# A fused two-layer transformer step: the roll layer in seven groups of four images and two of two, with spectra multiplied by three real products

## The chip, the cores and the metric

The kernel runs on one core of one Trainium2 chip. The metric is the device time of one execution in microseconds (us): 1072.96 is the median of 3 runs (1072.81 to 1073.27).

## What is computed

32 images give 36 patch tokens each, to which 32 text tokens are appended: S = 68 tokens per image, 2176 rows of 256 numbers, held as 17 tiles of 128 rows. Two layers follow, each an attention and a mixture of experts. The change is in the attention of the second layer, the "roll layer":

```
z    = softmax over s of (x @ W_A.T) / 4           # 16 heads, one weight per token
roll = zp[:, :, (i - j) % S] * tril                # a causal convolution over the 68 tokens
out  = einsum('bhij,bjhd->bihd', roll, x @ W_V.T)
h    = h + out @ W_O.T + b_O
```

## The kernel before

All stages are written out by hand for the five engines: PE (matmul), ACT and DVE (elementwise), POOL (gathers) and SP (DMA issue), tied by semaphores. `roll_layer` (line 1471) also finishes the mixture before it: POOL gathers the 8 expert rows of each token (136 indirect DMAs, line 1606), and DVE adds them into `h` (`combine`, line 1919).

The convolution is done in the frequency domain. `forward` (line 1646) multiplies the values of two images (a pair, 512 columns) by a cosine and a sine matrix (68x68), `forward_mix` (line 1658) does so for the softmax weights, `multiply` (line 1965) forms on DVE the four real products of the two complex spectra, and `invert` (line 1672) sums the four, each by its inverse matrix, in `po`.

The 32 images go in NG = 8 groups of GI = 4 images (two pairs each), one group a step, in a pipeline of three stages: in step `i` group `g1 = i-1` is normalised, turned (`turn("in")`), and its logits and values are computed; group `g2 = i-2` goes through `forward`, `multiply`, `invert` and `project`; group `g3 = i-3` is added to `h`, normalised again, turned (`turn("out")`), given its expert logits (`choose`) and written to DRAM by SP (lines 1554 and 1555). There are NG + 3 = 11 steps, 0 to 10; steps 9 and 10 have no `g1`. Step `i` also combines the gathered rows of the tiles of group `i`.

Each engine takes its instructions in the order written in its own loop over the steps (PE from line 1742, ACT from 1870, DVE from 1987). On PE there stand `fill`, `fill_values` and `fill_mid` (lines 1688 to 1705) between the stages: bf16 matmuls of 512 columns whose result nothing reads, 17 of them in a full step. POOL's gathers are paced by waits on PE's progress (`first_half`, `second_half`). An fp32 matmul shows as two records in the trace.

Of the kernel before, what the change touches and what calls it, by code (L numbers as in the profile page):

```python
# [71 lines left out]
def constants():  # L72
# [28 lines left out]
        "inv_re": (np.cos(turn).T * weight),  # L101
# [1369 lines left out]
def roll_layer(nc, a, k, r, wt, y_rows, shared_up, shared_down):  # L1471
# [8 lines left out]
    CP = 2 * S  # L1480
    YR = 4

    def tiles_in(g):
        if not 0 <= g < NG:
            return []
        return list(range(0 if g == 0 else 2 * g + 1, 2 * g + 3))

    def tiles_out(g):
        if not 0 <= g < NG:
            return []  # L1490
        return list(range(2 * g, NT if g == NG - 1 else 2 * g + 2))

    def pairs_out(g):
        ts = tiles_out(g)
        return [(ts[n] // 2, ts[n:n + 2]) for n in range(0, len(ts), 2)]
# [11 lines left out]
    with ExitStack() as st:  # L1507
# [9 lines left out]
        zf = sb("zf", [NF, 2, 2, GI, H])  # L1517
        v = sb("v", [S, 2, GI, D])
        term = sb("term", [NF, 2, 4, 2 * D])
# [23 lines left out]
        with nc.Block() as block:  # L1543
# [16 lines left out]
            def _(pool):  # L1560
# [4 lines left out]
                def first_half(g, kk):  # L1565
                    if kk == 1 and g >= 2:
                        pool.wait_ge(projected, pairs_out(g - 2)[-1][0] + 1)
# [43 lines left out]
            def _(pe):  # L1611
# [9 lines left out]
                def mix_logits(g):  # L1621
                    pe.wait_ge(turn_moved, turn_at["in", tiles_in(g)[-1]] + 1)
                    if g:
                        pe.wait_ge(zf_moved, g)
                    for c in range(DC):
                        mm = nc.tensor.matmul(pz[0:H, 0:GC], late["w_a"][:, c, :], xT[:, c, g * GC:(g + 1) * GC],
                                              start=(c == 0), stop=(c == DC - 1))
                    mm.then_inc(z_done, 1)

                def values(g, p):  # L1630
                    j = g * 2 + p
# [9 lines left out]
                def forward(g, p, part):  # L1641
                    n = (g * 2 + p) * 2 + part
                    pe.wait_ge(v_moved, g * 2 + p + 1)
                    if n >= 3:
                        pe.wait_ge(terms, 2 * (n - 2))
                    nc.tensor.matmul(pf[0:NF, n % 3, :], fwd[part], v[:, g % 2, 2 * p:2 * p + 2, :].rearrange("s b n -> s (b n)"),
                                     start=True, stop=True).then_inc(forwarded, 1)

                def turn_mix(g):
                    pe.wait_ge(z_normed, g + 1)  # L1650
                    for b in range(GI):
# [3 lines left out]
                def forward_mix(g):  # L1655
                    pe.wait_ge(zt_moved, g + 1)
                    for part in range(2):
                        mm = nc.tensor.matmul(pz[0:NF, (1 + part) * GI * H:(2 + part) * GI * H], fwd[part],
                                              zt[:, :, :].rearrange("s b m -> s (b m)"), start=True, stop=True)
                    mm.then_inc(zf_done, 1)  # L1660

                def invert(g, p):
                    j = g * 2 + p
                    pe.wait_ge(terms, (j + 1) * 4)
                    if j:
                        pe.wait_ge(out_moved, j)
                    for c in range(DC):
                        for b in range(2):
                            for i in range(4):
                                for half in range(2):  # L1670
# [3 lines left out]
                                        term[:, j % 2, i, lo:lo + P // 2], inv[i], start=(i == 0), stop=(i == 3))  # L1674
                    mm.then_inc(inverted, 1)

                def project(g, m, ts):
                    pe.wait_ge(out_moved, 2 * (g + 1))
                    if m:
                        pe.wait_ge(proj_added, m)  # L1680
                    for s, t in enumerate(ts):
# [12 lines left out]
                def fill_values(g, n):  # L1694
                    pe.wait_ge(v_moved, g * 2 + 2)
# [4 lines left out]
                def fill_mid(g, n):  # L1700
                    if not 0 <= g < NG:
# [40 lines left out]
                for i in range(STEPS):  # L1742
# [34 lines left out]
                    if has1:  # L1777
                        values(g1, 1)
# [8 lines left out]
                    if has2:  # L1787
                        invert(g2, 1)
                        fill_values(g1, 2)
                    if has1:  # L1790
                        turn_mix(g1)
                    for m, ts in pairs_out(g2):
                        project(g2, m, ts)
# [6 lines left out]
            def _(act):  # L1800
                def move_out(g, p):
                    j = g * 2 + p
# [4 lines left out]
                def move_mix(g):  # L1807
# [3 lines left out]
                    nc.scalar.activation(z[:, :, :].rearrange("m b s -> m (b s)"), pz[0:H, 0:GC], ACT.Copy,  # L1811
                                         scale=float(HD) ** -0.5).then_inc(z_moved, 1)

                def move_values(g, p):
                    if g >= 2:
                        act.wait_ge(forwarded, (g - 1) * 4)
                    act.wait_ge(v_done, g * 2 + p + 1)
# [27 lines left out]
                def exp(g):  # L1845
                    act.wait_ge(z_shifted, g + 1)
                    nc.scalar.activation(z[:, :, :], z[:, :, :], ACT.Exp).then_inc(exped, 1)

                def move_mix_turned(g):
                    act.wait_ge(z_turned, g + 1)  # L1850
                    nc.scalar.activation(zt[:, :, :].rearrange("s b m -> s (b m)"), pz[0:S, 0:GI * H], ACT.Copy)\
                        .then_inc(zt_moved, 1)

                def move_mix_forwarded(g):
                    act.wait_ge(zf_done, g + 1)
                    if g >= 2:
                        act.wait_ge(terms, (g - 1) * 8)
                    nc.scalar.activation(zf[:, g % 2, :, :, :].rearrange("f r b m -> f (r b m)"), pz[0:NF, GI * H:3 * GI * H],
# [11 lines left out]
                for i in range(STEPS):  # L1870
# [3 lines left out]
                    if has2 and not has1:  # L1874
                        move_out(g2, 0)
                        move_out(g2, 1)
# [18 lines left out]
                    if has1:  # L1895
                        move_values(g1, 1)
                        exp(g1)
                    if has2:
                        move_out(g2, 0)
                        move_out(g2, 1)  # L1900
# [5 lines left out]
            def _(dve):  # L1906
# [29 lines left out]
                def mix_shift(g):  # L1936
                    dve.wait_ge(z_moved, g + 1)
                    link(nc.vector.tensor_reduce(zpeak[:, :], z[:, :, :], AX.X, ALU.max))
                    nc.vector.tensor_tensor(z[:, :, :], z[:, :, :], zpeak[:, :].unsqueeze(2).broadcast_to([H, GI, S]),
                                            ALU.subtract).then_inc(z_shifted, 1)  # L1940

                def mix_norm(g):
                    dve.wait_ge(exped, g + 1)
                    link(nc.vector.tensor_reduce(zsum[:, :], z[:, :, :], AX.X, ALU.add))
                    link(nc.vector.reciprocal(zsum[:, :], zsum[:, :]))
                    nc.vector.tensor_tensor(z[:, :, :], z[:, :, :], zsum[:, :].unsqueeze(2).broadcast_to([H, GI, S]),
                                            ALU.mult).then_inc(z_normed, 1)

                def add_projected(m, ts):
                    dve.wait_ge(projected, m + 1)  # L1950
# [4 lines left out]
                def multiply(g, p):  # L1955
                    j = g * 2 + p
# [4 lines left out]
                    for i, part, zpart in ((0, 0, 0), (2, 0, 1), (1, 1, 1), (3, 1, 0)):  # L1961
                        n = j * 2 + part
                        dve.wait_ge(forwarded, n + 1)
                        weights = zf[:, g % 2, zpart, 2 * p:2 * p + 2, :].rearrange("f b m -> f (b m)")
                        mm = nc.vector.tensor_tensor(term[:, s, i, :].rearrange("f (m n) -> f m n", n=HD),
                                                     pf[0:NF, n % 3, :].rearrange("f (m n) -> f m n", n=HD),
# [21 lines left out]
                for i in range(STEPS):  # L1988
# [5 lines left out]
                    for m, ts in pairs_out(g3):  # L1994
                        add_projected(m, ts)
                    if has2 and not has1:
                        multiply(g2, 0)
                        multiply(g2, 1)
                        for t in outs:
                            dve.wait_ge(proj_added, t // 2 + 1)  # L2000
                            measure("out", t)
                        scale("out", outs)
                        continue
# [425 lines left out]
```

## Time and profile before

| | us |
|---|---|
| median of 3 runs | 1072.96 |
| the profiled execution, its own time | 1074.8 |
| its span, first to last instruction | 1073.0 |
| roll layer, from its first gather to its last DVE instruction | 634.5 to 875.1 |
| of it step 3 to the end | 718 to 875 |
| PE busy over the span | 939.0 (88%) |
| DVE busy | 582.3 (54%) |
| ACT busy | 412.1 (38%) |
| POOL busy | 519.4 (48%) |

Times in the rows are us from the start of the span. In a timeline row the first number is the start, the second the length until the last of its records ends; matmuls overlap, so the cost of a group is read from its start to the next group's start. The bracket gives the idle time before it on that engine and who ended it. PEclk is the granted TensorE clock: 1.00 is 2.4 GHz, 0.50 is 1.2 GHz.

### The profile page before, as it was taken

How to read it: one execution, taken by the hardware profiler on the slowest of the kernel's cores; microseconds unless marked ns; L12 is line 12 of the kernel's file. 1: busy time of each engine (PE TensorE's matmuls, PEld its weight loads, DVE VectorE, ACT ScalarE, POOL GpSimd, SP SyncE). 2: the span in 40 equal slices, each digit the busy share in tenths (PEclk: the TensorE clock that was granted, in tenths of full speed). 3: DMA queues.
4: the chain of work that ended last, by engine and by line, in shares of the span. 5: the costliest groups of instructions: out<-in, count | busy, mean ns of one | idle time of the engine just before them, and what ended most of it. 6: DMA issues, size and time to landing. Idle time of an engine off the chain costs nothing. (4 is left out here: it accounts for less than half of the span.)

```text
span 1073.0 us, 29482 instructions
## 1 busy us (share of the span) xinstructions
PE 939.0 (88%) x10318; PEld 741.5 (69%) x10318; DVE 582.3 (54%) x1439; ACT 412.1 (38%) x1094; POOL 519.4 (48%) x714
## 2 busy tenths in 40 slices
PE   8699999978824999999999986599999954999996
PEld 6457777767722888888888875255665634888895
DVE  1768888855995677533333325678877432111111
ACT  2357667743334343443434311233333222333331
POOL 0045565620603777777677617777772002343332
PEclk9879999979967999999999989789999976999998
DMA  7010000002003988887888723335463047466750
GB/s 253 2 44 2 0 0 0 1 2 84 1 0 109 307 267 271 279 243 214 254 261 253 231 80 103 103 104 140 122 214 125 21 153 261 138 224 236 282 154 25
DMA packets 79820, 149.28 MB, mean 139 GB/s; under 512 B 18892, under 2 KB 53327, under 8 KB 75760
## 3 DMA queue, kind: packets, MB, share of 16 engines
q1 hardware_dynamic: 34768, 77.15, 21.4%
q0 software_dynamic: 17712, 47.88, 15.7%
q10 hardware_dynamic: 27248, 23.09, 6.4%
q8 instruction: 50, 0.82, 0.3%
q14 instruction: 42, 0.34, 0.1%
HBM read 200.22 MB, written 31.73 MB: 216 GB/s over the span
## 5 line engine op out<-in xcount | busy, mean ns | idle before, releaser
L1311 POOL DMA_INDIRECT x_x<-m_x_rows,x_idx x170 | 165.8, 975 | 75.2 <-issue 35.9
L1337 PE MATMUL x_pup<-x_xt,x_w 128*128 128x128 f32 (+1 forms) x2176 | 184.7, 251 | 0.0
L1337 PEld LDWEIGHTS x_pup<-x_xt,x_w 128*128 128x128 f32 (+1 forms) x2176 | 168.7, 166 | 6.0 <-issue 5.9
L1606 POOL DMA_INDIRECT rl_y<-m_y_rows,rl_idx x136 | 132.8, 976 | 46.3 <-issue 36.9
L1407 DVE TENSOR_TENSOR x_hid<-x_gate,x_pup 128x128 f32<-128x128 f32 x170 | 48.9, 288 | 148.3 <-ACT x_gate L1379 144.3
L1351 PE MATMUL x_pdown<-x_w,x_hid 128*128 128x256 f32 (+1 forms) x408 | 104.2, 389 | 0.3 <-DVE x_y L1414 0.3
L1375 ACT ACTIVATE x_xt<-x_pturn 128x256 f32<-128x256 f32 x170 | 65.3, 384 | 88.9 <-PE x_pturn L1322 86.0
L434 POOL TENSOR_TENSOR wa_probs<-wa_probs,wa_peak 68x544 f32<-68x544 f32 x64 | 69.9, 1092 | 58.7 <-DVE wa_peak L576 58.7
L2365 DVE TENSOR_TENSOR x_y<-x_pdown,x_b 128x256 f32<-128x256 f32 x21 | 8.9, 425 | 151.3 <-PE x_pdown L2321 151.3
L2351 ACT ACTIVATE x_hid<-x_pup,x_b 128x128 f32<-128x128 f32 (+1 forms) x200 | 52.9, 356 | 93.3 <-PE x_pup L2304 93.1
L1379 ACT ACTIVATE x_gate<-x_pup 128x128 f32<-128x128 f32 x170 | 47.2, 278 | 93.5 <-PE x_pup L1337 92.8
L1322 PE MATMUL x_pturn<-cst,x_x 128*128 128x128 f32 x340 | 68.3, 283 | 9.2 <-DMA x_x<-m_x_rows,x_idx 9.2
L1919 DVE SCALAR_TENSOR_TENSOR h<-rl_y,m_wt,h 128x256 f32<-128x256 f32 x136 | 66.1, 486 | 16.8 <-DMA rl_y<-m_y_rows,rl_idx 12.6
L1414 DVE COPY x_y<-x_pdown 128x256 f32<-128x256 f32 x170 | 71.3, 420 | 2.0 <-PE x_pdown L1351 0.5
L1322 PEld LDWEIGHTS x_pturn<-cst,x_x 128*128 128x128 f32 x340 | 45.4, 143 | 36.8 <-issue 13.1
L2260 POOL DMA_INDIRECT out_h<-x_y,m_ids_out x21 | 21.2, 1008 | 91.4 <-DVE x_y L2368 85.7
L620 ACT ACTIVATE wa_probs<-wa_probs 68x544 f32<-68x544 f32 x64 | 42.1, 658 | 46.4 <-POOL wa_probs L434 46.3
L1296 POOL COPY x_idx<-m_ids 128x1 uint32 (+1 forms) x170 | 37.0, 218 | 42.0 <-POOLq L904 40.9
L572 DVE TENSOR_TENSOR wa_probs<-wa_scores,cst 68x544 f32<-68x544 f32 x64 | 46.0, 719 | 10.0 <-PE wa_scores L530 7.6
L2304 PE MATMUL x_pup<-x_xt,late_w 128*128 128x128 f32 x384 | 48.0, 286 | 3.2 <-ACT x_xt L2341 1.9
L2304 PEld LDWEIGHTS x_pup<-x_xt,late_w 128*128 128x128 f32 x384 | 46.9, 201 | 5.6 <-issue 3.7
L1351 PEld LDWEIGHTS x_pdown<-x_w,x_hid 128*128 128x128 f32 (+1 forms) x408 | 48.1, 173 | 3.9 <-DVE x_hid L1407 0.6
(329 smaller groups left out, 1886.8 us busy)
## 6 DMA issues: line engine op xcount, KB each, us to landing
x_w<-in_experts SPq DMA_DIRECT2D x204, 384.0 KB
late_w<-in_w SPq DMA_DIRECT2D x28, 1024.0 KB, 14.5
m_y_rows<-x_y ACTq DMA_DIRECT2D x170, 128.0 KB
xT<-in_w SPq DMA_DIRECT2D x12, 1024.0 KB, 6.2
xn<-in_w SPq DMA_DIRECT2D x10, 1024.0 KB, 10.7
h<-in_w SPq DMA_DIRECT2D x10, 1024.0 KB, 14.7
m_x_rows<-xn SPq DMA_DIRECT2D x34, 128.0 KB, 1.9
x_x<-m_x_rows,x_idx POOLq DMA_INDIRECT x170, 3.1
```

The source lines that it names most:

```text
L434: nc.gpsimd.tensor_tensor(probs[:, slot4, :, :], probs[:, slot4, :, :], peak[:, slot2, :].unsqueeze(2).broadcast_to([S, HC, S]), ALU.subtr ...
L1311: nc.gpsimd.indirect_dma_start(x[:, s, :], None, x_rows, bass.IndirectOffsetOnAxis(ap=idx[:, s:s + 1], axis=0))\
L1322: mm = nc.tensor.transpose(pturn[:, bank, c * P:(c + 1) * P], x[:, s, c * P:(c + 1) * P], ident)
L1337: mm = nc.tensor.matmul(pup[rows:rows + wide, bank, m * P + side * wide:m * P + (side + 1) * wide], w[:, lane, first:first + wide], xt[:, ...
L1351: mm = nc.tensor.matmul(pdown[rows, s % 2, 0:D], hid[:, s, rows], w[:, lane, UP:W], start=True, stop=True)
L1375: nc.scalar.activation(xt[:, s, :], pturn[:, bank, 0:D], ACT.Copy).then_inc(turn_moved, 1)
L1407: nc.vector.tensor_tensor(hid[:, s, :], gate[:, s, :], pup[:, bank, P:2 * P], ALU.mult)\
L1414: nc.vector.tensor_copy(y[:, s, :], pdown[:, s % 2, 0:D]).then_inc(down_moved, 1)
L1606: nc.gpsimd.indirect_dma_start(y[:, t % YR, kk, :], None, y_rows, bass.IndirectOffsetOnAxis(ap=idx[:, n:n + 1], axis=0))\
L1919: nc.vector.scalar_tensor_tensor(h[:, t, :], y[:, t % YR, kk, :], wt[:, t, kk:kk + 1], h[:, t, :], ALU.mult, ALU.add).then_inc(added, 1)
L2304: mm = nc.tensor.matmul(pup[rows:rows + wide, s, half, to:to + wide], w1[l][:, c, first:first + wide], xt[:, s, at:at + wide], start=(c == ...
L2351: ins = nc.scalar.activation(hid[:, s, f, side * wide:(side + 1) * wide], pup[:, s, f // HB, at:at + wide], ACT.Gelu, bias=b1[:, l, f:f + 1])
```

## The change

The groups are now `SIZES = [4]*7 + [2]*2`: nine groups, twelve steps, the last two groups of one pair each. The tiles of a group follow from the running sum of images. Each spectrum product is formed from three real products in place of four: `forward` makes three parts (sum, cosine, sine) of each pair, `forward_mix` three, `multiply` three, and `invert` sums three. Each part has its own bank of `pf`. `project` takes one wait and one increment per group. The fills return at once for the two groups of two. The weights of the next stage (`NG - 4` in SP's loop) are issued behind group 4's rows in place of group 3's. The table of constants holds two 68x68 matrices more.

```
@@ constants
-        "inv_re": (np.cos(turn).T * weight),
+        "fwd_sum": np.cos(turn) - np.sin(turn),
+        "fwd_diff": -np.sin(turn) - np.cos(turn),
+        "inv_sum": (np.cos(turn).T - np.sin(turn).T) * weight,
@@ roll_layer
-    fwd = [k["const"]("fwd_re"), k["const"]("fwd_im")]
-    inv = [k["const"]("inv_re"), k["const"]("inv_neg"), k["const"]("inv_im"), k["const"]("inv_im")]
-    GI = 4
-    NG = B // GI
+    fwd = [k["const"](n) for n in ("fwd_sum", "fwd_re", "fwd_im")]
+    fwd_mix = [k["const"](n) for n in ("fwd_re", "fwd_diff", "fwd_sum")]
+    inv = [k["const"](n) for n in ("inv_sum", "inv_im", "inv_neg")]
+    PARTS = len(inv)
+    GI, PAIR = 4, 2
+    SIZES = [4] * 7 + [2] * 2
...
                 def forward(g, p, part):
-                    n = (g * 2 + p) * 2 + part
-                    pe.wait_ge(v_moved, g * 2 + p + 1)
-                    if n >= 3:
-                        pe.wait_ge(terms, 2 * (n - 2))
-                    nc.tensor.matmul(pf[0:NF, n % 3, :], fwd[part], ...
+                    n = pair_of(g, p) * PARTS + part
+                    pe.wait_ge(v_moved, pair_of(g, p) + 1)
+                    if n >= PARTS:
+                        pe.wait_ge(terms, n - PARTS + 1)
+                    nc.tensor.matmul(pf[0:NF, part, :], fwd[part], ...
...
-                            for i in range(4):
+                            for i in range(PARTS):
...
                 def fill(g, n):
+                    if NG - 2 <= g < NG:
+                        return
...
                 def fill_values(g, n):
-                    pe.wait_ge(v_moved, g * 2 + 2)
+                    if NG - 2 <= g < NG:
+                        return
+                    pe.wait_ge(v_moved, pairs_through(g))
...
                 def fill_mid(g, n):
-                    if not 0 <= g < NG:
+                    if not 0 <= g < NG - 2:
                         return fill(g, n)
@@ PE, the loop over the steps
                     if has2:
-                        forward(g2, 0, 0)
-                        forward(g2, 0, 1)
-                        forward(g2, 1, 0)
+                        for part in range(PARTS):
+                            forward(g2, 0, part)
...
                     if has2:
-                        forward(g2, 1, 1)
+                        for p in halves(g2)[1:]:
+                            for part in range(PARTS):
+                                forward(g2, p, part)
                     if has2 and not has1:
                         fill(g2 + 1, 8)
-                        invert(g2, 0)
-                        fill(g2 + 1, 4)
-                        invert(g2, 1)
-                        fill(g2 + 1, 2)
-                        for m, ts in pairs_out(g2):
-                            project(g2, m, ts)
+                        for p in halves(g2):
+                            invert(g2, p)
+                            fill(g2 + 1, 3)
+                        project(g2)
@@ DVE, multiply
-                    for i, part, zpart in ((0, 0, 0), (2, 0, 1), (1, 1, 1), (3, 1, 0)):
-                        n = j * 2 + part
-                        dve.wait_ge(forwarded, n + 1)
+                    for part in range(PARTS):
+                        dve.wait_ge(forwarded, j * PARTS + part + 1)
```

The order of PE in the middle of a full step, before (`rl_pz` from L1626 are the logits, `rl_pv` the values, `rl_pf` the forward products, `rl_pt` the turns, `rl_po` from L1672 the inverse; bf16 512-column rows are fills):

```order
L1626 MATMUL rl_pz<-xT,late_w_a 16x272 x2
L1637 MATMUL rl_pv<-late_w_v,xT 68x256 x4
L1646 MATMUL rl_pf<-rl_v,cst 68x512
L1618 MATMUL rl_pt<-cst,xn 128x128 x2
L1705 MATMUL rl_pz<-m_chosen_b,m_before_b 128x512
L1618 MATMUL rl_pt<-cst,xn 128x128 x2
L1705 MATMUL rl_pz<-m_chosen_b,m_before_b 128x512
L1637 MATMUL rl_pv<-late_w_v,xT 68x256 x4
L1712 MATMUL rl_po<-late_wr,rl_x 128x8 x4
L1705 MATMUL rl_pz<-m_chosen_b,m_before_b 128x512 x2
L1672 MATMUL rl_po<-cst,rl_term 64x68 x32
```

And now (the lines of the file have moved by 17 to 22):

```order
L1643 MATMUL rl_pz<-xT,late_w_a 16x272 x2
L1654 MATMUL rl_pv<-late_w_v,xT 68x256 x4
L1663 MATMUL rl_pf<-rl_v,cst 68x512 x3
L1635 MATMUL rl_pt<-cst,xn 128x128 x2
L1727 MATMUL rl_pz<-m_chosen_b,m_before_b 128x512
L1635 MATMUL rl_pt<-cst,xn 128x128 x2
L1727 MATMUL rl_pz<-m_chosen_b,m_before_b 128x512
L1654 MATMUL rl_pv<-late_w_v,xT 68x256 x4
L1734 MATMUL rl_po<-late_wr,rl_x 128x8 x4
L1727 MATMUL rl_pz<-m_chosen_b,m_before_b 128x512 x2
L1690 MATMUL rl_po<-cst,rl_term 64x68 x24
```

The one forward product in the middle of the step has become three, with the three at the step's start left as they were in number, and each of the two inverses of a step has 24 matmuls in place of 32. The fills stand where they stood.

The first step with a group of two as `g1` (step 8, `g2` still a group of four), on PE now:

```order
L1635 MATMUL rl_pt<-cst,xn 128x128 x2
L1643 MATMUL rl_pz<-xT,late_w_a 16x136 x2
L1654 MATMUL rl_pv<-late_w_v,xT 68x256 x4
L1663 MATMUL rl_pf<-rl_v,cst 68x512 x3
L1635 MATMUL rl_pt<-cst,xn 128x128 x4
L1734 MATMUL rl_po<-late_wr,rl_x 128x8 x4
L1690 MATMUL rl_po<-cst,rl_term 64x68 x48
L1669 MATMUL rl_pz<-cst,rl_z 68x16 x2
L1700 MATMUL rl_pr<-late_b_o,cst 128x256
L1702 MATMUL rl_pr<-late_w_o,xT 128x256 x2
```

Before, step 8 read as a full step does, with its 17 fills. Now the fills are gone, one tile is turned in, one pair of values is computed, and the two inverses follow each other directly.

## Rows read from the trace of the kernel before

**Rows 1.** Timeline of PE in one step: start us, us, instruction, [idle before <-releaser].
```profile
742.39 0.38 PE L1618 MATMUL rl_pt<-cst,xn 128*128 128x128 f32 x2
...
743.34 0.41 PE L1618 MATMUL rl_pt<-cst,xn 128*128 128x128 f32 x2 [0.35 <-ACT xT L1838]
...
744.23 1.09 PE L1626 MATMUL rl_pz<-xT,late_w_a 128*16 128x272 f32 x4
...
747.03 1.02 PE L1646 MATMUL rl_pf<-rl_v,cst 68*68 68x512 f32 x2
...
752.36 2.13 PE L1672 MATMUL rl_po<-cst,rl_term 68*64 68x68 f32 x64
...
754.41 0.61 PE L1705 MATMUL rl_pz<-m_chosen_b,m_before_b 128*128 128x512 bf16 x2
...
761.33 0.41 PE L1658 MATMUL rl_pz<-rl_zt,cst 68*68 68x64 f32 x4
...
761.58 0.60 PE L1697 MATMUL rl_pv<-m_chosen_b,m_before_b 128*128 128x512 bf16 x2
```

**Rows 2.** Timeline of DVE and ACT, the start of the next step.
```profile
762.50 0.16 DVE L1933 SCALAR_TENSOR_TENSOR rl_shift<-rl_mv,rl_rstd 128x2 f32<-128x2 f32 x1 [4.04 <-ACT rl_rstd L1826]
...
762.70 1.09 ACT L1832 ACTIVATE xn<-h,rl_shift,rl_rstd 128x256 f32<-128x256 f32 x2 [0.23 <-DVE rl_shift L1933]
...
764.40 2.48 DVE L1965 TENSOR_TENSOR rl_term<-rl_pf,rl_zf 68x512 f32<-68x512 f32 x4
```

**Rows 3.** Timeline of POOL, its last gather.
```profile
811.93 1.20 POOL L1606 DMA_INDIRECT rl_y<-m_y_rows,rl_idx  x1 [0.30 <-issue]
```

**Rows 4.** Busy time by engine over one step: length, PE, PEld, DVE, ACT, POOL, PEclk, DMA.
```profile
762.00:784.00 22.00, 21.26 (x210) 13.35 (x209) 17.29 (x40) 7.37 (x21) 16.82 (x18) 1.00 0.48 127
```

**Rows 5.** Timeline of PE from the last full step to the end of the layer.
```profile
828.59 2.74 PE L1646 MATMUL rl_pf<-rl_v,cst 68*68 68x512 f32 x6
...
846.98 0.70 PE L1682 MATMUL rl_pr<-late_b_o,cst 128*128 128x256 f32 x2
...
849.67 0.59 PE L1697 MATMUL rl_pv<-m_chosen_b,m_before_b 128*128 128x512 bf16 x2
...
850.78 3.63 PE L1646 MATMUL rl_pf<-rl_v,cst 68*68 68x512 f32 x8
...
854.25 1.89 PE L1692 MATMUL rl_pz<-m_chosen_b,m_before_b 128*128 128x512 bf16 x8
...
865.44 0.67 PE L1682 MATMUL rl_pr<-late_b_o,cst 128*128 128x256 f32 x2 [0.87 <-DVE h L1952]
...
866.81 0.38 PE L1618 MATMUL rl_pt<-cst,xn 128*128 128x128 f32 x2
```

**Rows 6.** Timeline of the SyncE queue: first weight load and last row write of the layer.
```profile
791.71 0.49 SPq L1550 DMA_DIRECT2D late_w<-in_w  x1
...
872.79 0.45 SPq L1555 DMA_DIRECT2D m_h_rows<-h  x1
```

**Rows 7.** Waits of the SyncE queue from 850 us on: total us, times, longest us.
```profile
SPq L1543 <- DMA m_h_rows<-h: 3.3, 1, 3.3
```

**Rows 8.** The page, section 6 (DMA issues): count, KB each, us to landing.
```profile
late_w<-in_w SPq DMA_DIRECT2D x28, 1024.0 KB, 14.5
```

**Rows 9.** Timeline of PE, beside two falls of its clock.
```profile
697.73 0.69 PE L1618 MATMUL rl_pt<-cst,xn 128*128 128x128 f32 x2 [3.66 <-ACT xn L1832]
...
704.81 1.02 PE L1646 MATMUL rl_pf<-rl_v,cst 68*68 68x512 f32 x2
...
873.27 1.51 PE L1712 MATMUL rl_po<-late_wr,rl_x 128*128 128x8 f32 x12
```

**Rows 10.** Busy time by engine, as rows 4, for stretches beside both falls.
```profile
697.00:700.00 3.00, 2.13 (x7) 1.00 (x7) 2.44 (x5) 1.79 (x4) 2.23 (x3) 0.50 0.38 115
...
874.00:874.50 0.50, 0.50 (x7) 0.50 (x7) 0.00 (x0) 0.00 (x0) 0.00 (x0) 0.93 0.31 105
874.50:875.00 0.50, 0.50 (x3) 0.24 (x3) 0.18 (x1) 0.00 (x0) 0.00 (x0) 0.50 0.00 0
```

More of the change, by code:

```diff
@@ L1474, in roll_layer @@
     ident = k["const"]("ident")
-    fwd = [k["const"]("fwd_re"), k["const"]("fwd_im")]
-    inv = [k["const"]("inv_re"), k["const"]("inv_neg"), k["const"]("inv_im"), k["const"]("inv_im")]
-    GI = 4
-    NG = B // GI
+    fwd = [k["const"](n) for n in ("fwd_sum", "fwd_re", "fwd_im")]
[4 more added lines that the diff above has]
+    SIZES = [4] * 7 + [2] * 2
+    assert sum(SIZES) == B
+    NG = len(SIZES)
+    FROM = [sum(SIZES[:g]) for g in range(NG + 1)]
     GC = GI * S
-    CP = 2 * S
+    CP = PAIR * S
     YR = 4
@@ L1485, in tiles_in @@
             return []
-        return list(range(0 if g == 0 else 2 * g + 1, 2 * g + 3))
+        return list(range(-(-FROM[g] * S // P), -(-FROM[g + 1] * S // P)))
     def tiles_out(g):
@@ L1490, in tiles_out, with halves, pair_of, pairs_through @@
             return []
[L1491 to L1495, printed above, removed]
+        return list(range(FROM[g] * S // P, FROM[g + 1] * S // P))
+    def halves(g):
+        return range(SIZES[g] // PAIR)
+    def pair_of(g, p):
+        return FROM[g] // PAIR + p
+    def pairs_through(g):
+        return FROM[g + 1] // PAIR
+    def cols_of(g):
+        return slice(FROM[g] * S, FROM[g + 1] * S)
+    assert all(len(tiles_out(g)) <= 2 for g in range(NG))
     STEPS = NG + 3
@@ L1650, in turn_mix @@
                     pe.wait_ge(z_normed, g + 1)
[L1651 removed]
+                    for b in range(SIZES[g]):
                         mm = nc.tensor.transpose(pz[0:S, b * H:(b + 1) * H], z[:, b, :], ident[0:H, 0:H])
@@ L1673, in invert, with project @@
                                         po[half * (P // 2):(half + 1) * (P // 2), (c * 2 + b) * S:(c * 2 + b + 1) * S],
-                                        term[:, j % 2, i, lo:lo + P // 2], inv[i], start=(i == 0), stop=(i == 3))
+                                        term[:, j % 2, i, lo:lo + P // 2], inv[i], start=(i == 0), stop=(i == PARTS - 1))
                     mm.then_inc(inverted, 1)
[L1677 to L1681, printed above, removed]
+                def project(g):
+                    pe.wait_ge(out_moved, pairs_through(g))
+                    if g:
+                        pe.wait_ge(proj_added, g)
+                    for s, t in enumerate(tiles_out(g)):
                         nc.tensor.matmul(pr[:, s, :], ident, late["b_o"][:, :], start=True, stop=False)
@@ L1777, in _ @@
                     if has1:
-                        values(g1, 1)
+                        for p in halves(g1)[1:]:
+                            values(g1, p)
                     for t in outs:
@@ L1787, in _ @@
                     if has2:
-                        invert(g2, 1)
-                        fill_values(g1, 2)
+                        for p in halves(g2)[1:]:
+                            invert(g2, p)
+                            fill_values(g1, 2)
                     if has1:
                         turn_mix(g1)
-                    for m, ts in pairs_out(g2):
-                        project(g2, m, ts)
+                    if has2:
+                        project(g2)
                     if has1:
@@ L1874, in _ @@
                     if has2 and not has1:
-                        move_out(g2, 0)
-                        move_out(g2, 1)
+                        for p in halves(g2):
+                            move_out(g2, p)
                         root("out", outs)
@@ L1895, in _ @@
                     if has1:
-                        move_values(g1, 1)
+                        for p in halves(g1)[1:]:
+                            move_values(g1, p)
                         exp(g1)
                     if has2:
-                        move_out(g2, 0)
-                        move_out(g2, 1)
+                        for p in halves(g2):
+                            move_out(g2, p)
                     if has1:
@@ L1993, in _ @@
                         scale("in", tiles_in(g1))
-                    for m, ts in pairs_out(g3):
-                        add_projected(m, ts)
+                    if outs:
+                        add_projected(g3)
                     if has2 and not has1:
-                        multiply(g2, 0)
-                        multiply(g2, 1)
+                        for p in halves(g2):
+                            multiply(g2, p)
+                        dve.wait_ge(proj_added, g3 + 1)
                         for t in outs:
-                            dve.wait_ge(proj_added, t // 2 + 1)
                             measure("out", t)
@@ L2019, in _ @@
                     if has2:
-                        multiply(g2, 1)
+                        for p in halves(g2)[1:]:
+                            multiply(g2, p)
                     if has1:
```

72 lines of the change are left out of this document (41 added, 31 removed).

## The prediction, made before the changed kernel had run

> **What bounds the kernel now.** The chain of waits that ended last lies in the expert stage behind the roll layer, so it says nothing of the change. I read the timeline of each engine inside the layer instead, then the busy time by engine of one step, then the clock.
>
> A full step takes 850.78 - 828.59 = 22.19 us from one step's first `forward` to the next one's [rows 5]. In a step PE is busy 21.26 of 22.00 us [rows 4]. It waits for 0.35 us behind the first turn in, until ACT has moved the tile [rows 1], and as long behind the first turn out; there is no other gap. DVE is busy 17.29 of the 22.00 us [rows 4] and stands still for 4.04 us until ACT gives it `rstd` [rows 2]; ACT stands behind PE's `forward_mix`, which ends PE's step. POOL's last gather is issued at 811.93 [rows 3], 0.30 us behind the one before it, and 63 us before the layer ends. So **PE's own list, fills included, sets the length of a step**: what is added to it is paid in full, what is taken from DVE is not seen.
>
> **The steps with a group of four: dearer.** Prices are from starts. Four `forward` products are 8 records and take 854.25 - 850.78 = 3.47 us [rows 5], 0.434 a record. An inverse is 64 records and takes 754.41 - 752.36 = 2.05 us [rows 1], 0.032 a record. `forward_mix` is 4 records in 761.58 - 761.33 = 0.25 us [rows 1], 0.06 a record.
> - `forward`: two pairs by one product more, 4 records, +1.73 us.
> - `invert`: twice 16 records fewer, -1.03 us.
> - `forward_mix`: one product more, 2 records, +0.12 us.
>
> Together +0.82 us a step. Steps 2 to 7 pay it (groups 0 to 5 in `forward`): **+4.9 us**. Step 2 pays too, though it begins late behind a gather: once PE starts its turns at 697.73 [rows 9] it runs on to the step's end.
>
> DVE saves one of four products a pair, 2.48 / 4 = 0.62 us [rows 2]. That goes into its wait of 4.04 us and is worth nothing. Moved or longer at no cost: the weights for the next stage are now issued a group later (before: from 791.71 [rows 6]), landing in 14.5 us [rows 8] where some 40 us are left; without that cover the layer's end would wait for the rest. ACT's copy of the mixed spectra grows by half; it runs under fills. The larger table of constants lands in the first stage, before its first reader.
>
> **The short end.** From step 8 on groups are short and have no fills, so PE's list no longer covers the round through ACT. Where one PE instruction needs what ACT must move from the one before, the pair costs 743.34 - 742.39 = 0.95 us in place of the 0.22 of a turn [rows 1]: 0.73 of waiting a round. I add work and rounds.
>
> Step 8 (before: 22.19). PE's work: six records of `forward` twice 2.60, turn in 0.22, logits half of 1.02 (744.23 to the values) is 0.51, values 747.03 - 744.23 - 1.02 = 1.78 [rows 1], two turns out 0.44, two `choose` 0.9 (of 1.51 for three [rows 9], two thirds and a little off for the overlap), two inverses of 48 records 3.08, `project` 849.67 - 846.98 = 2.69 [rows 5], the turns of the weights and `forward_mix` 0.43: 15.25. Rounds: turn in, turns out, between the inverses 0.73 each, the second `choose` 0.33, the move before `project` 0.6: 3.1. Together 18.35.
>
> Step 9 (before: 866.81 - 850.78 = 16.03 [rows 5], with two inverses, two `project`s and 14 fills). Now `g1` is the last group of two and `g2` has one pair: work 2.60 + 0.22 + 0.51 + 1.78 + 0.44 + 0.9 + 1.54 + 1.35 (`project` of one tile) + 0.37 = 9.7. Rounds: 0.73, then the turns out, which are late: ACT must normalise two tiles (1.09 [rows 2]) and move logits and values first, behind a DVE `scale` that stands behind `multiply`. I take 1.4 there, between 0.73 and 2.1. With 0.33 and 0.65: 3.1. Together 12.8.
>
> Step 10 and 11: `forward` 2.60, eight fills, the inverse, three fills, `project` of two tiles: 2.60 + 1.83 + 1.54 + 0.7 + 2.69 = 9.35. Then the last batch: the sum into `h`, measuring, `rstd`, normalising, row writes. Before, that ran from 866.81 to the end of the last issue at 872.79 + 0.45 = 873.24: 6.43 us with three tiles [rows 5, 6]. With two tiles it is one normalisation (0.55), one measuring (0.6) and two issues less, less what overlaps, and the sum of two tiles is now in it: 5.3.
>
> Sum of the end: 18.35 + 12.8 + 9.35 + 5.3 = 45.8; before 873.24 - 828.59 = 44.65 [rows 5, 6]. **+1.1 us**: the fills that go are eaten by the waits that come and by one step more. SP waits 3.3 us for that last write [rows 7], and the layer ends with it, so it stands for the end.
>
> **The clock.** PE runs at 1.00 through all full steps [rows 4]. After 3.66 us without work PE restarted at 0.50, the 1.2 GHz level, between 697 and 700 [rows 9, 10]. From there to the `forward` at 704.81 it took 7.08 us; the same stretch at full clock takes 747.03 - 742.39 = 4.64 [rows 1, 9]. So one fall costs 2.4 us of dense work. But a fall needs no long pause: at 874.5 the clock went to 0.50 with PE busy all the half microsecond before, on the twelve small `choose` records behind turns with gaps of 0.4 us [rows 9, 10]. In step 9 turns out, `choose` and a gap of 1.4 us stand together with no fill between them, the same mix. The trace of before has no such stretch inside the layer, so I bound it: 0 if the clock holds, 2.4 for a fall in dense work, 4.8 for one in step 8 as well. I take one fall, in step 9, nearest to the row at 874. A quarter of step 9 is waiting (3.1 of 12.8), which a slow clock doesn't lengthen: **+1.8 us**.
>
> The Trainium skill has two sections on this in "TensorE: Matmul & The Clock Gate". "HAM oscillation — how this bites in real kernels" ties the fall to long waits for data between groups of matmuls; by that alone a gap of 1.4 us would leave the clock up and the sum at 1079.0. "A second HAM failure mode: psum-queue depth-cycling" says that frequent short idles between groups also make the clock swing; by that the sum is the one I forecast. The fall at 874 agrees with the second.
>
> **The sum.** +4.9 +1.1 +1.8 = +7.8 us in the profiled span (1073.0; that execution took 1074.8 in all, 1.8 above the span). The parts outside the layer don't change, so the median of the runs moves as much: 1072.96 + 7.8 = **1080.8**.
>
> **Rivals.**
> - *The clock holds* (first section of the page; for it: the longest gap I add is under half of 3.66 us; against: 874). +6.0: 1079.0.
> - *It falls in step 8 too*, around the turns out and `choose`. Against: the inverses behind them are dense. +9.6: 1082.6.
> - *The short steps run without waits.* For: DVE has spare time, and PE may find each move already done. Then 6.2 us of rounds go: 4.9 + 1.1 - 6.2 = -0.2, 1072.8, no change. Against: the turn needs ACT's copy, and one copy is 0.73 away in every step of the trace.
> - *The other side: DVE, not PE, paces the steps.* Then three products in place of four take 0.62 us from each of the 14 pairs of the first seven groups, -8.7, and the extra `forward`s lie beside them: with the end +1.1, 1065.4. It decides where DVE's wait for `rstd` is nothing. Against: that wait is 4.04 us, and PE's whole idle is 0.7 a step.
>
> Over 0.2% (2.1 us, about what a measurement of this kernel can tell from no change) is faster below 1070.8 and slower above 1075.1.
>
> **How the numbers follow.** One fall of the clock 0.42, none 0.32, two 0.12, no waits 0.09, DVE 0.05. The first three are slower: 0.86, of which I take 0.01 off because all three could be 4 us too dear. Faster 0.07: the DVE case and a little of the one without waits. Same 0.08. The first three hold more than 8 in 10, from 1079.0 to 1082.6; the unknown rounds (some 3 us below, if half of them are covered) and the bounds of the clock stretch this to 1076.0 to 1084.0.
>
> **What the profile after would show.** Full steps of 23.0 us from `forward` to `forward`, PE without gaps but the two of 0.35, six records where two stood in the middle of the step and 48 in an inverse of some 1.54 us; DVE's wait for `rstd` grown from 4.04 to some 6 us. From step 8 on, steps of about 18, 13 and 9 us, PE with gaps of 0.6 to 1.5 us, and a stretch at 0.50 behind the turns out of step 9. I am wrong on the steps if they stay at 22.2 or shrink; on the end if from the `forward` of step 8 to the last row write there are not 45 to 49 us; on the clock if it stays at 1.00 up to the last `choose`.

## Result: slower by 1.35%, and the clock falls twice

| | before | after |
|---|---|---|
| median of 3 runs, us | 1072.96 (1072.81 to 1073.27) | 1089.43 (1082.34 to 1090.88) |
| ratio, 95% interval | | 1.0135 [1.0106, 1.0163] |
| span of the profiled execution, us | 1073.0 | 1087.6 |
| first `forward` of the layer, us | 691.34 | 690.21 |
| first `forward` of step 8, us | 828.59 | 832.78 |
| end of the last row write's issue, us | 873.24 | 887.27 |

The forecast was 1080.8 with a range of 1076.0 to 1084.0. The sign is right; the time is 5.4 us above the range. Ratios leave out two executions of the later runs that were far slower than the rest, of 4652.83 and 1163.24 us. The page of the changed kernel, sections 1 and 2 (busy tenths and granted clock in 40 slices):

```profile
PE 950.8 (87%) x10098; PEld 745.1 (69%) x10098; DVE 575.1 (53%) x1430; ACT 413.2 (38%) x1102; POOL 518.0 (48%) x714
PE   8699999978734999999999983899999965999996
PEclk9889999969967999999999997899999776999998
```

PE has 220 records fewer than before and is busy 11.8 us longer. Records differ in price, so that proves nothing yet, but the row of the clock shows where to look: in it the 32nd digit (843 to 870 us) is 7; before, the 32nd (832 to 858 us) was 9.

Timeline of PE in the changed kernel, one full step (compare [rows 1]):

```profile
740.32 2.74 PE L1663 MATMUL rl_pf<-rl_v,cst 68*68 68x512 f32 x6
...
743.85 0.41 PE L1635 MATMUL rl_pt<-cst,xn 128*128 128x128 f32 x2 [0.35 <-ACT xT L1862]
...
747.53 2.74 PE L1663 MATMUL rl_pf<-rl_v,cst 68*68 68x512 f32 x6
750.11 0.38 PE L1635 MATMUL rl_pt<-cst,xn 128*128 128x128 f32 x2
...
754.58 1.67 PE L1690 MATMUL rl_po<-cst,rl_term 68*64 68x68 f32 x48
756.17 0.61 PE L1727 MATMUL rl_pz<-m_chosen_b,m_before_b 128*128 128x512 bf16 x2
...
762.63 0.53 PE L1676 MATMUL rl_pz<-rl_zt,cst 68*68 68x64 f32 x6
763.00 0.60 PE L1719 MATMUL rl_pv<-m_chosen_b,m_before_b 128*128 128x512 bf16 x2
763.43 1.02 PE L1663 MATMUL rl_pf<-rl_v,cst 68*68 68x512 f32 x2
```

The step takes 763.43 - 740.32 = 23.11 us, 0.92 more than before's 22.19 [rows 5]; the only waits are still the two of 0.35 behind a first turn. The forecast had 23.0. Then the short end, where the forecast failed. Timeline of PE from step 8 to the end of step 10, and the last row write of SP:

```profile
832.78 2.74 PE L1663 MATMUL rl_pf<-rl_v,cst 68*68 68x512 f32 x6
...
842.09 0.41 PE L1635 MATMUL rl_pt<-cst,xn 128*128 128x128 f32 x2 [0.57 <-ACT rl_x L1867]
842.33 1.25 PE L1734 MATMUL rl_po<-late_wr,rl_x 128*128 128x8 f32 x8
843.51 1.66 PE L1690 MATMUL rl_po<-cst,rl_term 68*64 68x68 f32 x48
845.76 2.91 PE L1690 MATMUL rl_po<-cst,rl_term 68*64 68x68 f32 x48 [0.59 <-ACT xT L1827]
...
853.93 2.77 PE L1663 MATMUL rl_pf<-rl_v,cst 68*68 68x512 f32 x6
...
861.01 0.41 PE L1635 MATMUL rl_pt<-cst,xn 128*128 128x128 f32 x2 [0.89 <-ACT rl_x L1867]
861.25 1.25 PE L1734 MATMUL rl_po<-late_wr,rl_x 128*128 128x8 f32 x8
862.43 2.56 PE L1690 MATMUL rl_po<-cst,rl_term 68*64 68x68 f32 x48
...
868.84 5.37 PE L1663 MATMUL rl_pf<-rl_v,cst 68*68 68x512 f32 x6
874.00 3.19 PE L1712 MATMUL rl_pz<-m_chosen_b,m_before_b 128*128 128x512 bf16 x8
877.12 1.67 PE L1690 MATMUL rl_po<-cst,rl_term 68*64 68x68 f32 x48
...
881.97 0.38 PE L1635 MATMUL rl_pt<-cst,xn 128*128 128x128 f32 x2
```
```profile
886.82 0.45 SPq L1572 DMA_DIRECT2D m_h_rows<-h  x1
```

The two inverses of step 8 are the same 48 records, yet one takes 1.66 us and the next 2.91. The six `forward` records of step 10 take 5.37 us where those of step 8 take 2.74, and the eight fills behind them take 3.19 where eight took 1.89 in the kernel before [rows 5]. No wait stands inside these groups; they run slowly. Busy time by engine of these stretches (us, PE busy and records, PEld, DVE, ACT, POOL, PEclk, DMA share, GB/s):

```profile
845.00:848.00 3.00, 2.41 (x47) 2.30 (x45) 2.80 (x6) 0.40 (x1) 0.00 (x0) 0.65 0.00 0
848.00:851.00 3.00, 2.74 (x18) 2.17 (x16) 0.61 (x2) 0.48 (x2) 0.00 (x0) 0.50 0.00 0
851.00:854.00 3.00, 3.00 (x16) 2.47 (x15) 0.00 (x0) 0.00 (x0) 0.00 (x0) 0.71 0.00 0
860.00:863.00 3.00, 1.99 (x30) 1.79 (x30) 1.29 (x5) 1.44 (x4) 0.00 (x0) 0.99 0.52 175
863.00:875.00 12.00, 11.74 (x61) 6.53 (x56) 2.55 (x5) 0.72 (x3) 0.00 (x0) 0.50 0.00 0
875.00:878.00 3.00, 3.00 (x35) 1.47 (x35) 0.45 (x2) 0.00 (x0) 0.00 (x0) 0.73 0.00 0
```

PEclk is at 0.50, the 1.2 GHz level, from about 846 to 852 us and again from 863 to 876 us. Steps 8, 9, 10 and the last batch take 21.15, 14.91, 13.13 and 5.3 us; the forecast had 18.35, 12.8, 9.35 and 5.3. The layer ends 14.0 us later than before, of the span's 14.6.

### The profile page after: what moved, and what is told of

The parts are those of the page before. It is cut to its first block and busy times, and to the rows that moved or that the text cites. A ratio compares the mean times of both kernels' runs of the same rounds, so it can differ in the third digit from the quotient of the medians.

```text
span 1087.6 us, 29062 instructions
## 1 busy us (share of the span) xinstructions
PE 950.8 (87%) x10098; PEld 745.1 (69%) x10098; DVE 575.1 (53%) x1430; ACT 413.2 (38%) x1102; POOL 518.0 (48%) x714
## 5 line engine op out<-in xcount | busy, mean ns | idle before, releaser
L1324 PEld LDWEIGHTS x_pturn<-cst,x_x 128*128 128x128 f32 x340 | 45.3, 143 | 36.5 <-issue 13.1
```

The source lines that it names most:

```text
L1324: mm = nc.tensor.transpose(pturn[:, bank, c * P:(c + 1) * P], x[:, s, c * P:(c + 1) * P], ident)
```

## The experiments

Two theories stood against each other. *Clock:* the short steps lose the clock because their fills are gone, and its falls are the excess. *Rounds:* the waits between PE and ACT in short steps cost more than was priced, whatever the clock. In every experiment "the end" means the time from step 8's first `forward` to the end of the last row write's issue: 44.65 us before, 54.49 in the first trace of the changed kernel.

**The changed kernel again**, unedited, twice, each beside other runs on the same chip.

> The changed kernel again, unedited. Clock theory: what is lost beyond the longer full steps is lost in the three short steps, where the clock falls to 0.50. A fall need not come in every execution at the same place, so the times scatter: some near 1082, some near 1090, and in the profiled one the length of steps 8 to 10 (54.5 us in the first trace with the last batch, 832.78 to 887.27) goes with how long the clock is at 0.50. Rival, rounds theory: the waits between engines in the short steps cost the time at any clock; then the end is 53 to 55 us long whatever the clock shows, and the times scatter no more than the kernel before does (0.5 us).

> The changed kernel again, unedited, beside the two runs above on the same chip: 1083 to 1091, two falls of the clock in the last three steps, the end 51 to 55 us long.

Measured: 1084.16 (1083.14 to 1086.5), ratio 1.0109 [1.0094, 1.0125]; and 1084.61 (1083.78 to 1085.78), ratio 1.0119 [1.0105, 1.0132]. The ends were 51.00 and 51.08 us, steps 8 to 10 of the first 21.05, 15.09 and 9.57. Busy time by engine beside its two falls:

```profile
846.00:853.00 7.00, 6.31 (x57) 5.53 (x58) 3.07 (x8) 0.76 (x3) 0.00 (x0) 0.52 0.00 0
863.00:870.00 7.00, 6.74 (x64) 5.72 (x64) 0.81 (x3) 0.67 (x3) 0.00 (x0) 0.52 0.01 2
```

Two falls again, at the same two places, but the second ends at about 870 and not at 876, so step 10 takes 9.57 us and not 13.13. It is some 6.7 us shorter; work done at half speed there loses half of that, and the end is 54.49 - 51.00 = 3.49 us shorter. So the time goes with the clock, while the waits are the same, and the rival's end of 53 to 55 us did not come. The untraced times scatter less than the clock theory expected (1083.14 to 1086.5). In the first three runs two of 1089.43 and 1090.88 stand beside one of 1082.34; the traced one of 1089.43 is the one with the long second fall.

**All fills put back into the short groups.**

```
 def fill(g, n):            # and the same in fill_values
-    if NG - 2 <= g < NG:
-        return
 def fill_mid(g, n):
-    if not 0 <= g < NG - 2:
+    if not 0 <= g < NG:
```

> The changed kernel with the fills put back into the two short groups. Clock theory: PE has no stretch of small records and waits without a fill between, the clock stays at 1.00 from step 8 to the last choose; step 8 about 19.4 us, step 9 about 13.5 to 14, step 10 about 9.4, last batch 5.3, together 47.6 in place of 54.5: about 1082, 7 us under the changed kernel's 1089.4, still some 9 above the kernel before. Rival, rounds theory: the waits through ACT are the cost and fills only add to PE's list: 1089 to 1092.

Measured: 1082.81 (1081.27 to 1083.46), ratio 1.0098 [1.0082, 1.0113]. Busy time by engine in the end:

```profile
843.00:883.00 40.00, 38.35 (x354) 24.72 (x353) 15.27 (x42) 11.23 (x33) 0.00 (x0) 1.00 0.10 33
```

The clock stays at 1.00, and the end is 48.74 us (steps 19.94, 14.25, 9.25, 5.3). The expectation had 47.6. Against the unedited kernel on the same chip the traced end is 2.3 us shorter; the medians differ by 1.35 with intervals that overlap, so a gain in time is not shown. The falls are the missing fills' doing, but most of what the clock gives back goes into the fills themselves: PE's list in a short step is long again.

**Only the fills beside the weak places put back:** behind the turns out, behind `choose` and behind the first inverse. The edit is that of `fill_mid` alone.

> The changed kernel with only a part of the fills back in the two short groups: those beside the turns out, behind the choose records and behind the first inverse; none beside the turns in, behind the last inverse and around forward_mix. Clock theory, with the place of the fall: it is the turns out, choose and the wait for ACT behind the inverse that lose the clock, so these fills are enough: clock 1.00 up to the last choose, and the end is 48.7 us (all fills back) less about 1.4 us in step 8 and 1.1 in step 9: 46.2, and 1080.5 in all. If every fill of a short step counts, the clock falls in step 9 at least, and the time is 1083 to 1085, as without any.

Measured: 1079.51 (1077.47 to 1082.83), ratio 1.0058 [1.0036, 1.0080]. PE from step 8 on:

```profile
833.56 2.74 PE L1663 MATMUL rl_pf<-rl_v,cst 68*68 68x512 f32 x6
...
844.74 1.67 PE L1690 MATMUL rl_po<-cst,rl_term 68*64 68x68 f32 x48
846.57 0.38 PE L1727 MATMUL rl_pz<-m_chosen_b,m_before_b 128*128 128x512 bf16 x1 [0.16 <-issue]
847.00 1.66 PE L1690 MATMUL rl_po<-cst,rl_term 68*64 68x68 f32 x48
...
852.18 2.77 PE L1663 MATMUL rl_pf<-rl_v,cst 68*68 68x512 f32 x6
...
861.13 1.66 PE L1690 MATMUL rl_po<-cst,rl_term 68*64 68x68 f32 x48
...
865.17 2.77 PE L1663 MATMUL rl_pf<-rl_v,cst 68*68 68x512 f32 x6
...
874.45 0.38 PE L1635 MATMUL rl_pt<-cst,xn 128*128 128x128 f32 x2
```
```profile
843.00:880.00 37.00, 33.86 (x330) 22.97 (x334) 15.26 (x41) 11.12 (x33) 0.00 (x0) 1.00 0.10 32
```

The clock holds, both inverses take 1.66 us, and the steps are 18.62, 12.99 and 9.28 us; with 5.3 for the last batch the end is 46.19, against 46.2 expected. There are six of these fills a step (the expectations further down count five). Four stand where PE would wait for ACT anyway. The two behind `choose` lie on PE's list: the first inverse starts 844.74 - 833.56 = 11.18 us into step 8, and 843.51 - 832.78 = 10.73 in the first trace without fills, both before any fall; in step 9 it is 861.13 - 852.18 = 8.95 and 862.43 - 853.93 = 8.50. So some 0.9 us of the 46.19 are fills, and an estimate of the unedited kernel's end at full clock is 45.3. With a clock that holds, the short steps are thus what the forecast had priced (18.35, 12.8, 9.35, 5.3): the rounds theory falls.

**Two fills a short step, both behind `choose`.**

```
 for t in outs:
     choose(t)
 fill_mid(g1, 2)
+if NG - 2 <= g1 < NG:
+    pe.wait_ge(z_moved, g1 + 1)
+    for _ in range(2):
+        nc.tensor.matmul(pz[:, :], r["before_b"][:, :], filler, ...)
```

> The changed kernel with two fills a short step, both behind choose, and no other in these steps. If it is the small choose records by themselves that lose the clock, these two fills hold it: end of about 46 us, as with the five fills a step beside the turns out, choose and the first inverse (46.2), and about 6 us under the unedited kernel on the same chip. If the sum of waits in the step counts (behind the turns and between the inverses, 0.5 to 0.9 us each), the clock falls as without fills: end of 51 to 55 us, within 2 us of the unedited kernel.

Measured: 1083.46 (1079.19 to 1087.28), ratio 1.0106 [1.0083, 1.0128]. In the traced execution, the second inverse of step 8 and busy time by engine:

```profile
844.48 1.66 PE L1690 MATMUL rl_po<-cst,rl_term 68*64 68x68 f32 x48 [0.59 <-ACT xT L1831]
```
```profile
840.00:850.00 10.00, 8.55 (x128) 7.33 (x130) 5.41 (x14) 1.80 (x7) 0.00 (x0) 1.00 0.01 2
860.00:865.00 5.00, 4.67 (x26) 3.25 (x22) 0.42 (x1) 0.72 (x3) 0.00 (x0) 0.66 0.00 0
```

Step 8 held the clock (18.62 us), step 9 lost it for some 3.4 us (14.30), and the end was 47.72. The runs scatter over 8 us, and the interval meets that of the unedited kernel. In this trace two fills behind `choose` are not enough in step 9: what stands behind the turns and the inverse counts too. Step 8 says something else: its waits are those of the unedited kernel, 0.59 us before the second inverse among them, and the inverse still takes 1.66 and not 2.91. Those waits alone do not bring the clock down. What the other five executions did cannot be told from their times, so this run says less than it was meant to.

**Three products alone:** the kernel before, eight groups of four, with the changed kernel's `fwd`, `fwd_mix`, `inv` and three terms. One of the places:

```
-    for i, part, zpart in ((0, 0, 0), (2, 0, 1), (1, 1, 1), (3, 1, 0)):
+    for part in range(PARTS):            # PARTS = 3; GI = 4, NG = 8 stay
```

> The kernel before with three real products only, its eight groups of four kept. PE-list theory: each full step is 23.1 us in place of 22.2, as in the changed kernel, from step 2 to 8, and no short step and no new fall of the clock: 7 times 0.9 and a little for step 9 (four records of forward more, 32 of invert fewer, +0.7): 1079 to 1080. Rival, DVE paces: steps of 21 to 22 us and 1065 to 1073.

Measured: 1079.13 (1078.77 to 1081.62), ratio 1.0067 [1.0054, 1.0081], 7.3 us. Full steps are 23.11 us from `forward` to `forward`, the rest behind step 8 is 0.8 longer, and the clock stays at 1.00 from 736 to 875 us. DVE has a quarter less to multiply and nothing comes of it: PE's list sets the step.

**The regrouping alone:** seven groups of four and two of two, no fills in the short ones, four products. Against the kernel before, in short:

```
-    NG = B // GI
+    SIZES = [4] * 7 + [2] * 2            # PARTS = 2: cosine and sine, four terms
```

> The changed kernel's groups (seven of four, two of two, no fills in the short ones) with the four products of the kernel before. PE-list theory: full steps of 22.2 us, so no cost until step 8. Clock theory: the two falls are due to the missing fills, not to the products, and stay; the end then costs what it costs in the changed kernel, about +9 us: 1081 to 1084. Rival: the falls come of the three products (their dense forward and shorter invert); then the end is within 2 us of that of the kernel before: 1073 to 1075.

Measured: 1081.77 (1081.6 to 1084.24), ratio 1.0098 [1.0082, 1.0113]. Full steps are 22.19 us, the end 53.83, and the clock:

```profile
838.00:848.00 10.00, 9.70 (x82) 8.27 (x82) 2.78 (x7) 0.47 (x2) 0.00 (x0) 0.50 0.01 2
858.00:868.50 10.50, 10.24 (x60) 5.75 (x55) 3.13 (x6) 0.69 (x3) 0.00 (x0) 0.52 0.01 2
```

The same two falls, ten microseconds each. They come without the three products.

**The regrouping alone, with the fills of the third experiment** (`fill_mid` put back).

> Seven groups of four and two of two with the four products of the kernel before, and the five fills a short step beside the turns out, choose and the first inverse. Clock theory: with the clock at 1.00 the regrouping by itself is neutral: steps of 17.8, 12.6, 8.9 and 5.3 us for the last batch (18.62, 12.99, 9.28 and 5.3 with three products, less two forward records and plus sixteen inverse records a pair), together 44.6, as the 44.65 of the kernel before; ratio 0.998 to 1.002. Rival: the rounds through ACT cost what was predicted too low, and the end is 47 us or more, ratio 1.002 to 1.004.

Measured: 1073.82 (1072.1 to 1077.18), ratio 1.0013 [1.0002, 1.0024]. The clock holds at 1.00; the end is 45.77 us, 1.1 above the expected 44.6 and 1.2 below the rival's 47. Timeline of PE in step 9, and busy time by engine in the end:

```profile
850.31 0.44 PE L1633 MATMUL rl_pt<-cst,xn 128*128 128x128 f32 x2 [0.86 <-ACT xn L1855]
851.80 0.41 PE L1633 MATMUL rl_pt<-cst,xn 128*128 128x128 f32 x2 [1.05 <-ACT rl_x L1866]
```
```profile
834.00:872.00 38.00, 33.55 (x381) 23.40 (x386) 18.07 (x47) 10.73 (x33) 0.00 (x0) 1.00 0.10 33
```

Step 9 is the miss (13.74 for 12.6): its turns out wait 0.86 us for ACT to normalise and 1.05 for `rl_x`, where the version with three products had one wait of 0.89. The regrouping with a clock that holds costs 0.1%, where without fills it costs 1.0%.

The measured ratios together, each to the kernel before in the same series:

| | eight groups of four | short groups, no fills | short groups, fills at the weak places |
|---|---|---|---|
| four products | 1 | 1.0098 | 1.0013 |
| three products | 1.0067 | 1.0109 to 1.0135 | 1.0058 |

**Fewer fills in the full steps of the kernel before.** If PE's list sets the step, a fill that covers no wait can go. Six go (two of four between the inverses, the two ahead of `forward_mix` and the two behind it), then the two behind `choose` as well, then the six in the version with three products.

```
                     if has1:
                         fill_mid(g1, 2)
-                        fill_values(g1, 2)
...
                     if has1:
-                        fill_values(g1, 2)
                         forward_mix(g1)
-                        fill_values(g1, 2)
```

> The kernel before with six fills of a full step left out: two of the four between the inverses, two ahead of forward_mix and two behind it. PE-list theory: none of them covers a wait (ACT's copy between the inverses ends 0.4 us before the second inverse starts), so a step is six times 0.217 = 1.3 us shorter, 20.9 us, over seven steps 9 us: 1062 to 1064, with the clock at 1.00. Clock theory's rival: a step then has dense work enough only at its start, the clock falls as in the short steps, and the time is no better than before, up to 10 us worse. Rival, another engine takes over (DVE's round or POOL's sixteen gathers of 0.95 + 0.30 = 1.25 us, 20.0 a step): steps of 21.5 to 22.2 us and 1067 to 1073.

> The kernel before with those six and the two fills behind choose left out. PE-list theory: 1.75 us a step, steps of 20.4 us, just above POOL's sixteen gathers (20.0): 1059 to 1062 with the clock at 1.00. Clock theory: behind the small choose records now stands a wait or the inverse and no fill, the place where the short steps lost the clock, so this one falls where the one with six fewer holds: steps of 23 to 26 us, 1075 to 1095.

> Eight groups of four with three real products, and the same six fills left out. PE-list theory: steps of 23.1 - 1.3 = 21.8 us, seven times 0.4 less than the kernel before, 0.8 more in the last steps: about 1070, 9 us under three products with all fills. If the clock falls without these fills, 1080 or more; the three products are then no better at holding it than the four.

Measured against the kernel before: six fewer, ratio 0.9974 [0.9961, 0.9988], steps of 21.01 us; eight fewer, 0.9947 [0.9928, 0.9966], 1067.38 (1065.6 to 1069.73), steps of 20.57; three products and six fewer, 0.9990 [0.9977, 1.0004], 1072.62 (1070.35 to 1075.52), steps of 21.94. The clock stayed at 1.00 in the full steps, also without the two behind `choose`: the clock theory's expectation for that run was wrong. Three products gain, by the ratios, some 8 us from six fewer fills, where 9 were expected. On the kernel before, steps shorter by 1.18 and 1.62 us would make 8.3 and 11.3 over seven steps; by the ratios they brought 2.8 and 5.7. Step 7 did not get shorter. Timeline of DVE and PE in step 7, six fills fewer, busy time by engine behind it, and DVE's wait for the same gather in the kernel before:

```profile
799.04 4.18 DVE L1916 SCALAR_TENSOR_TENSOR h<-rl_y,m_wt,h 128x256 f32<-128x256 f32 x8 [6.11 <-DMA rl_y<-m_y_rows,rl_idx]
805.35 0.69 PE L1618 MATMUL rl_pt<-cst,xn 128*128 128x128 f32 x2 [2.96 <-ACT xn L1829]
```
```profile
805.35:808.35 3.00, 2.86 (x8) 1.12 (x9) 2.93 (x8) 1.59 (x5) 2.08 (x4) 0.50 0.45 143
```
```profile
798.76 4.15 DVE L1919 SCALAR_TENSOR_TENSOR h<-rl_y,m_wt,h 128x256 f32<-128x256 f32 x8 [0.68 <-DMA rl_y<-m_y_rows,rl_idx]
```

PE has caught up with the gathers: DVE waits 6.11 us for one, PE 2.96 for the rows made from it (4.85 with eight fewer), and restarts at 0.50 for about 3 us. The last gather is issued at 811.06 us, hardly earlier than before's 811.93 [rows 3]. In the kernel before, DVE already waits 0.68 us at that place: POOL issues its gathers back to back from 658 us on, one every 1.27 us on average, although waits on PE's progress stand in its list. A group needs 136 / 8 = 17 of them, an estimate of 21.6 us: less than a step of 22.19, more than one of 21.01 (the expectation counted 16, 20.0 us). So POOL's gathers take over as the bound: PE draws level with them, and step 7 takes 25.28 and 26.84 us. With three products and six fills fewer the steps of 21.94 stay above 21.6, and step 7 has no such wait. The version with eight fills fewer beats the kernel before by 0.5%, and the changed kernel by 1.6 to 1.9% if ratios from different chips are set against each other.

## Why the prediction was wrong

The sum, term by term, against two traces of the changed kernel (us; the clock's term is the end less the 46.19 measured with fills and a clock that holds):

| term | predicted | first trace | traced again |
|---|---|---|---|
| full steps, 2 to 7 | +4.9 | +5.32 | +5.28 |
| the end at 1.00 | +1.1 | +1.54 | +1.54 |
| clock | +1.8 | +8.30 | +4.81 |
| start of the layer's first `forward` | 0 | -1.13 | -0.42 |
| behind the layer | 0 | +0.57 | +0.49 |
| span | +7.8 | +14.6 | +11.7 |

With the estimate of 45.3 for that end without fills, the end at 1.00 is +0.6 and the clock's term 9.2 and 5.7.

- **Full steps: right.** 23.11 us for 23.0. `forward` adds 1.72 (predicted 1.73), `forward_mix` 763.00 - 762.63 = 0.37 for 0.25, so 0.12 as predicted. An inverse of 48 records takes 1.59 and not 1.54: the sixteen records that go were worth 0.46 and not 0.51. Three products alone, with 1.0067, show the term by itself. DVE's waits in a step came to some 6 us as forecast, though not as one longer wait for `rstd`. Timeline of DVE in the changed kernel, the waits of the step from 786.55:

```profile
787.10 0.16 DVE L1962 SCALAR_TENSOR_TENSOR rl_shift<-rl_mv,rl_rstd 128x2 f32<-128x2 f32 x1 [3.72 <-ACT rl_rstd L1850]
...
791.37 0.16 DVE L1962 SCALAR_TENSOR_TENSOR rl_shift<-rl_mv,rl_rstd 128x2 f32<-128x2 f32 x1 [0.48 <-ACT rl_rstd L1850]
...
800.67 0.43 DVE L1975 TENSOR_REDUCE rl_zsum<-rl_z 16x4 f32<-16x272 f32 x1 [1.84 <-ACT rl_z L1872]
```

The third is for the softmax's exponentials, which DVE now reaches before ACT has made them; before, the wait for `rstd` was 4.04 [rows 2].
- **The end at full clock: right.** 46.19 with fills, an estimate of 45.3 without, for 45.8; each step is within 0.3 us. The rounds priced at 0.73 from [rows 1] were good enough.
- **The clock: mis-sized, the step that failed.** "I take one fall, in step 9" was the forecast, and "it falls in step 8 too" a rival at 0.12 with the reason "the inverses behind them are dense". In all three traces of the unedited kernel it falls in both steps; in the first the second inverse of step 8 is the very group in which it starts, behind a wait of 0.59 us. Dense records on the way did not protect it. So a term of +1.8 measured +8.30 and +4.81. The price of one fall was about right where the fall was as short as that of [rows 9]: steps 8 and 9 of the second trace are 2.4 and 2.1 us longer than with a clock that holds (2.9 and 2.6 without the fills' 0.45), for 2.4. What had no term was a fall that lasts: in the first trace the clock stayed at 0.50 over 13 us, through `forward` and eight fills of step 10, all dense, and that step alone lost 3.85 us. The upper bound of 4.8 would have given 1083.8, inside the range and near the two later medians; no bound held the first.
- **The other rivals.** DVE does not pace the steps, and the short steps do wait. The clock did not hold.
- **The sections cited.** The Trainium skill, "TensorE: Matmul & The Clock Gate", section "A second HAM failure mode: psum-queue depth-cycling", tells of a kernel of bf16 matmuls whose clock swings with frequent short idles. The runs agree with it in part: no wait in the short steps is longer than 0.89 us, and the clock falls in both. But with fills beside them waits of 0.89 and 1.05 us remain, and it holds. By the Trainium skill's section "HAM oscillation — how this bites in real kernels" alone it would have held.

Not settled: whether the small records between the waits bring the clock down by themselves or only together with the waits, since no run took the waits away and left the records as they are. Nor why the second fall lasted 13 us once and 7 twice in the same program, and 10 with four products. Only traced executions show how long a fall lasts. The untraced runs of 1090.88 and 1082.34 us, with mean granted clocks of 0.928 and 0.933, may be such a long and a short one; that is argued, not shown.

## What to carry to other kernels

Work that only keeps TensorE's clock up looks free to remove; ask of each piece whether it stands in a wait (then it costs nothing, and may be what holds the clock) or on the engine's list (then it costs its own length). Price a clock fall by how often and how long it can happen, and let the range reach to two falls and to one that lasts. Where one engine's list sets a step, relief for another engine is worth nothing; and before shortening that list, look how far ahead the next supplier is, here the gathers.

## What the runs showed of the hardware

- The clock stayed at 0.50 for 13 us while PE was busy 11.74 of 12.00 us; in the same kernel another fall ended after about 7 us.
- It fell with no wait over 0.59 us in the step (step 8 of the first trace), behind turns, eight `choose` records and an inverse of 64-column weights; one or two 512-column bf16 fills at each of these places, six a step, kept it at 1.00, with waits of up to 1.05 us left in the step.
- With the same waits in step 8 as in the kernel without fills, two fills behind `choose` kept it at 1.00 in that step, in the one trace there is.
- In full steps eight fills of 17 could go without a fall; there the granted clock fell only at a wait of 2.96 us or more for rows of a late gather.
- POOL issued its gathers back to back at 1.27 us each on average; at 17 a group, steps of 21.01 us ran into a wait of 6.11 us for one of them, and steps of 21.94 did not.
